# A residual product that reads its projected rows straight from PSUM, in a block of attention and routed experts on one core

## The chip, the cores and the metric

The kernel runs on one core of a Trainium2 chip. The metric is the device time of one launch in microseconds (us), the median of several launches. The engines are named as in the profile: PE (TensorE; PEld is its weight load), DVE (VectorE), ACT (ScalarE), POOL (GpSimd) and SP (SyncE, which here only issues transfers).

## What is computed

Eight sequences of 256 tokens, 256 wide, go through an attention block and a feed-forward block, each between two layer norms and with a residual:

```python
x = x + layernorm(attention(layernorm(x), Wq, Wk, Wv, Wo, b_out))   # 32 heads of 8, 8 key heads, causal, rotary
x = x + layernorm(experts(layernorm(x), ...))                       # top 2 of 8 experts, and 2 shared ones, inner width 640
```

The change lies between the attention's output projection `ctx @ Wo + b_out` and the first residual sum. Because the program centres `Wo` and `b_out` beforehand, the projected rows have mean zero, and the norm needs their mean square alone: `x1 = x + y * (mean(y*y) + eps) ** -0.5`.

## The kernel before

The 2048 tokens are 16 tiles of 128 (index `i`, two for each of 8 sequences). All is in fp32 or in sums of two fp32r or three bf16 parts. Each engine has its own instruction list, and all five lists are written from one list of steps, `plan()`: an engine takes from it the steps that concern it, in that order, and waits on semaphores. So the place of a step in `plan()` sets what it stands behind on every engine that has a part in it. The places come from tables: `FRONT`, `FRONT0`, `FRONT1` for the steps ahead of attention (layer norm, projection, rotary turn, splitting in bf16 parts, transposes by DMA; `FRONT0` is for the first sequence, `FRONT1` for the second), `BACK` for those behind it, `TOPS`, `WHOLE` and `LEAD` for the running start of the maxima, `ORDER` for the order within one of the 64 attention steps. A number in `BACK` is a time in quarters of an attention step. `WARM` gives the number of idle matmuls that PE does behind certain steps of the start.

An attention step `n` is one key head of one sequence with its 4 query heads, 256 by 256 scores. PE makes a first set of scores (`early` and `late`, 7 steps ahead) from which DVE takes the maxima (`tops`, L1078, and `lates`, L1083); POOL turns these into three bf16 parts (`neg`), PE transposes them (`turn`), ACT copies them out and SP writes them beside the queries (`turned`, L1629); then PE makes the scores again with the maxima in them (`pass2`), ACT takes the exponential (`exp`, L930), POOL cuts the causal triangle (L1511), and PE multiplies by the values (`weigh`).

Four steps after a sequence's heads, for each tile `i`, comes what the change touches. PE projects (`b_out`) into a PSUM bank. ACT (`b_taken`) copies the 256 columns to the SBUF tile `YY` and then squares the bank in place with a running sum into `BN`; the bank is free after the squares. POOL (`b_dev`, L1539 and L1541) makes `RS = (sum/256 + eps) ** -0.5`. DVE (`b_add`, L1359) writes `X1 = YY * RS + X1`, and takes the statistics of the second norm (`b_stats2`, L1363, and `b_dev2`, L1366). ACT (`b_norm2`, L948) writes the normalised row to `YY` again, which SP stores for the experts' gather and PE transposes (`b_turn2`) for ACT (`b_high`) and DVE (`b_low`, L1370, tile `XL`).

`banks()` gives out the PSUM banks in the order of `plan()`. During attention the banks 3 to 6 go round as a ring for `early`, `late` (two neighbouring banks), `turn`, `back`, `b_turn`, `b_out`, `b_turn2`, `b_route` and `f_qkv`. PE waits before each until the engine that read the bank last has freed it.

At the start SP issues, from one queue, the transposes by DMA of queries and keys (`q`, L1614, two halves each, and `k`, L1620) and, in the step `k` of the second tile of a sequence, the loads of a later sequence (`XT` L1583, `X` L1579). The first `early` scores need the transposes of tile 0; the first `late` ones need those of tile 0 and of tile 1.

The attention takes the first 250 us of the trace. Behind it PE runs the two shared and the eight routed experts (`up`, `down`), with gathers by POOL's queue.

## Time and profile before

| | us |
|---|---|
| median of 3 launches | 660.78 |
| lowest and highest | 659.98 and 661.0 |
| the profiled launch, as timed | 666.35 |
| its span in the trace | 664.6 |

So 1.75 us of the profiled launch lie around its span, and it was 5.57 us above the median. All positions below are microseconds from the start of the span. Over the span PE was busy for 93%, DVE 80%, ACT 64% and POOL 50%; the mean granted clock of PE was 0.975. A matmul's end is modelled, so PE can show as busy without being at its peak, and an engine's share over the whole span says little here, since attention and experts have different limits: the stretches are to be read one by one. Where a row of the order of time ends in brackets, the engine stood idle before it for so long, and the arrow names what ended it.

### The profile page before, as it was taken

Reading aid. Unit: us, or ns where it says so; the run is one execution under the profiler, and the core shown is the slowest. Engines: PE = TensorE matmul, PEld = TensorE weight load, DVE = VectorE, ACT = ScalarE, POOL = GpSimd, SP = SyncE. Lnnn points to the kernel's source line nnn. Section 1 sums busy time; section 2 is a strip of 40 time slices with the busy share of each in tenths; the row PEclk is TensorE's granted clock in tenths of the full one; section 3 lists DMA queues with packets and bytes.
Section 4 is the critical chain, followed back from the end, with each engine's and each line's share of the span. In section 5 each row is a group of like instructions: output and inputs, shape, how many; then the busy total and the mean of one; then the engine's idle time right before and its main releaser. Section 6 shows DMA issues by size and latency. Waiting matters only on the chain.

```text
span 664.6 us, 14332 instructions
## 1 busy us (share of the span) xinstructions
PE 617.6 (93%) x5400; PEld 514.7 (77%) x5400; DVE 528.7 (80%) x1071; ACT 425.0 (64%) x798; POOL 335.5 (50%) x529
## 2 busy tenths in 40 slices
PE   8778889899989879999979999999999999999995
PEld 6634556566656548888879999999999999888884
DVE  5679999999988734579768888888887888557886
ACT  3436798988988874542256777777876787422222
POOL 3136688787867661100354454545454430078854
PEclk9966899999999999999999999999999999999999
DMA  3973544557450000000375786777776764032311
GB/s 94 158 150 56 99 81 77 120 93 179 100 92 24 13 17 9 17 1 1 126 269 179 242 277 233 242 251 247 240 279 219 265 229 151 25 91 78 97 53 63
DMA packets 79795, 87.08 MB, mean 131 GB/s; under 512 B 54736, under 2 KB 69200, under 8 KB 79728
## 3 DMA queue, kind: packets, MB, share of 16 engines
q0 software_dynamic: 11872, 54.53, 25.0%
q1 hardware_dynamic: 67440, 31.12, 20.8%
q8 instruction: 43, 0.70, 0.4%
q10 hardware_dynamic: 416, 0.52, 0.3%
q14 instruction: 24, 0.20, 0.1%
HBM read 63.87 MB, written 9.31 MB: 110 GB/s over the span
## 4 chain that ended last, share of the span: by engine, by line
PE 66%; DVE 20%; issue 5%; ACT 3%; POOL 3%; another core or an unknown queue 1%; DMA 1%; SPq 0%; POOLq 0%; DVEq 0%; ACTq 0%
PE PS L559 63%; DVE NM L1083 6%; DVE NM L1078 3%; PE PS L768 1%; POOL PF L1511 1%; ACT PF L930 1%; DVE RR L1042 1%; DVE RB L1036 1%; DVE RA L1035 1%; DVE X L1359 1%; PE PS L570 1%; ACT WH L877 1%; DMA WQ<-in_wqkv 1%; DVE RB L1037 1%
## 5 line engine op out<-in xcount | busy, mean ns | idle before, releaser
L1297 DVE TENSOR_TENSOR HF<-SS,PS 128x256 f32<-128x256 f32 (+2 forms) x141 | 68.7, 487 | 72.3 <-PE PS L559 32.6
L1378 DVE TENSOR_TENSOR WL<-RAW,WH 128x768 fp32r<-128x768 f32 x125 | 118.4, 958 | 5.7 <-ACT WH L877 5.2
L976 ACT ACTIVATE SS<-PS 128x256 f32<-128x256 f32 (+2 forms) x141 | 62.0, 439 | 86.7 <-PE PS L559 72.3
L559 PE MATMUL PS<-WH,HH 128*128 128x256 f32 x355 | 103.6, 292 | 3.8 <-DVE HL L1392 2.9
L877 ACT ACTIVATE HH<-HF 128x256 fp32r<-128x256 f32 (+1 forms) x120 | 58.0, 483 | 72.6 <-DVE HF L1297 58.5
L877 ACT ACTIVATE WH<-RAW 128x768 fp32r<-128x768 f32 x125 | 103.4, 841 | 0.0
L1511 POOL TENSOR_SCALAR_AFFINE_SELECT PF<-PF 128x512 f32<-128x512 f32 x128 | 83.9, 679 | 36.5 <-ACT PF L930 36.5
L559 PE MATMUL PS<-WL,HH 128*128 128x256 f32 x355 | 100.3, 283 | 0.0
L559 PE MATMUL PS<-WH,HL 128*128 128x256 f32 x355 | 100.3, 283 | 0.0
L930 ACT ACTIVATE PF<-PS 128x1536 f32<-128x1536 f32 x64 | 92.8, 1450 | 10.8 <-PE PS L559 10.0
L559 PE MATMUL PS<-XGL,WH 128*128 128x256 f32 x320 | 91.0, 284 | 0.0
L559 PE MATMUL PS<-XGH,WH 128*128 128x256 f32 x320 | 90.9, 284 | 0.0
L559 PE MATMUL PS<-XGH,WL 128*128 128x256 f32 x320 | 90.9, 284 | 0.0
L559 PEld LDWEIGHTS PS<-WH,HH 128*128 128x128 f32 x355 | 67.6, 190 | 7.5 <-ACT HH L877 4.1
L1083 DVE TENSOR_REDUCE NM<-PS 128x14 f32<-128x896 f32 x64 | 69.1, 1082 | 4.4 <-PE PS L559 4.0
L559 PEld LDWEIGHTS PS<-WL,HH 128*128 128x128 f32 x355 | 67.5, 190 | 1.9
L559 PEld LDWEIGHTS PS<-WH,HL 128*128 128x128 f32 x355 | 67.7, 191 | 0.0
L1483 POOL DMA_INDIRECT RAW<-in_wa,WIDX x23 | 22.7, 985 | 83.3 <-DVE WL L1378 40.8
L559 PE MATMUL PS<-XH,WH 128*128 128x512 f32 x160 | 64.1, 401 | 0.0
L559 PE MATMUL PS<-XL,WH 128*128 128x512 f32 x160 | 63.3, 396 | 0.0
L559 PE MATMUL PS<-XH,WL 128*128 128x512 f32 x160 | 63.1, 394 | 0.0
L1392 DVE TENSOR_TENSOR HL<-HF,HH 128x256 fp32r<-128x256 f32 (+1 forms) x120 | 62.0, 517 | 0.2 <-ACT HH L877 0.2
(214 smaller groups left out, 1520.2 us busy)
## 6 DMA issues: line engine op xcount, KB each, us to landing
ys<-YO SPq DMA_DIRECT2D x16, 256.0 KB
RAW<-in_wsh SPq DMA_DIRECT2D x4, 768.0 KB, 4.9
XT<-in_xt SPq DMA_DIRECT2D x8, 256.0 KB, 3.4
X<-in_x SPq DMA_DIRECT2D x8, 256.0 KB, 3.3
xn<-YY SPq DMA_DIRECT2D x16, 128.0 KB, 1.7
out<-X SPq DMA_DIRECT2D x15, 128.0 KB
ys<-YO SPq DMA_DIRECT2D x7, 128.0 KB
RAW<-in_wsh SPq DMA_DIRECT2D x2, 384.0 KB, 4.7
```

The source lines that it names most:

```text
L559: return eng.matmul(o, l, r, start=start, stop=stop, skip_group_check=True)
L570: t = eng.transpose(bank(c, 128 * k, 128 * k + 128), src[:, 128 * k:128 * k + 128], idn)
L877: return eng.activation(o, i, ACT.Copy)
L930: eng.activation(PF[:, i % 3, :], PS[:, 0:1536], ACT.Exp, scale=SCALE).then_inc(expd, 1)
L976: eng.activation(ss, both(i, bank(b))[0], ACT.Silu).then_inc(free[b] if dense(i) else silu, 1)
L1078: eng.tensor_reduce(o[:, :, 3:8:2], bank(c, 0, 384).rearrange("p (a v t) -> p a v t", a=2, v=3), AXX, ALU.max, negate=True).then_inc(free[ ...
L1083: eng.tensor_reduce(o[:, :, 9:16], bank(c, 0, 1024).rearrange("p (a v t) -> p a v t", a=2, v=8)[:, :, 0:7, :], AXX, ALU.max, negate=True). ...
L1297: eng.tensor_tensor(hf, ss, both(c, bank(b))[1], ALU.mult).then_inc(free[b], 1)
L1378: eng.tensor_tensor(WL[q % 2][:, c], RAW[raw_of(q)][:, c], WH[q % 2][:, c].bitcast(F32), ALU.subtract).then_inc(w_lo, 1)
L1392: eng.tensor_tensor(HL[:, i % 4, 0:n], HF[:, i % 2, 0:n], HH[:, i % 4, 0:n].bitcast(F32), ALU.subtract).then_inc(h_lo, 1)
L1483: eng.indirect_dma_start(RAW[raw_of(q)][:, 768 * lo:768 * hi], None, (wa, wb, wc)[k], bass.IndirectOffsetOnAxis(ap=WIDX[:, q - 1:q], axis= ...
L1511: eng.affine_select(out=o, in_=o, pattern=[[0, 4], [1, 128]], base=0, channel_multiplier=-1, compare_op=ALU.is_ge, fill=0.0).then_inc(zero ...
```

## The change

ACT's copy of the projected rows goes. Its squares are now written to the upper half of the same bank (columns 256 to 511), so that the lower half keeps the rows; DVE's `b_add` reads them there and frees the bank, which before the squares did. POOL's `b_dev` waits for the squares by their own semaphore. The waits for the room in `YY` go from `b_taken` to `b_norm2`, the step that still writes it. `banks()` keeps a bank out of the ring from `b_out` to `b_add`.

```diff
 elif what == "b_taken":                                    # ACT
     made(e, ("b_out", i))
+    eng.activation(bank(c, 256, 512), bank(c, 0, 256), ACT.Square, accum_out=BN[:, 16 + i, 0:1]).then_inc(b_y, 1)
+elif what == "b_norm2":
+    e.wait_ge(c_nb, i + 1)
     made(e, ("b_turn2", i - 2))
     e.wait_ge(d_xn[i % 2], 16 * (i // 2))
-    copy(YY[:, i % 2, :], bank(c, 0, 256)).then_inc(b_y, 1)
-    eng.activation(bank(c, 0, 256), bank(c, 0, 256), ACT.Square, accum_out=BN[:, 16 + i, 0:1]).then_inc(free[c], 1)
-elif what == "b_norm2":
-    e.wait_ge(c_nb, i + 1)
...
 elif what == "b_add":                                      # DVE
+    c, k = use["b_out", i]
+    made(e, ("b_out", i))
+    e.wait_ge(b_y, i + 1)
     e.wait_ge(b_rs, i + 1)
-    e.wait_ge(b_y, i + 1)
-    eng.scalar_tensor_tensor(out=X1[:, i, :], in0=YY[:, i % 2, :], scalar=RS[:, 16 + i:17 + i], in1=X1[:, i, :],
-                             op0=ALU.mult, op1=ALU.add).then_inc(b_x1, 1)
+    eng.scalar_tensor_tensor(out=X1[:, i, :], in0=bank(c, 0, 256), scalar=RS[:, 16 + i:17 + i], in1=X1[:, i, :],
+                             op0=ALU.mult, op1=ALU.add).then_inc(free[c], 1)
...
 elif what == "b_dev":                                      # POOL
-    read(e, ("b_out", i))
+    e.wait_ge(b_y, i + 1)
...
-LAGS = (9, 10)
+LAGS = (10, 10)
-WARM = {"mean": (9,), "f_qkv": (1, 6, 8, 21), "early": (8, 0, 3, 0, 0, 2, 0), "late": (2,)}
+WARM = {"mean": (14,), "f_qkv": (1, 6, 10, 18), "early": (8, 0, 2, 0, 0, 0, 3), "late": (0,)}
-TOPS = (-8, -7, -7, -5, -5, -2, -1)
+TOPS = (-9, -7, -7, -6, -6, -2, -1)
-ORDER = "a 2 b x d l s1 s0 s2 m0 m1 t w T m2 v W V m3 s3"
+ORDER = "a x 2 b d l s1 s0 m0 s2 t w T m1 v m2 V W s3 m3"
```

The numbers of `FRONT`, `FRONT0`, `FRONT1`, `BACK` and `WHOLE` change too, most of them by one to five. What they move is best seen in the lists of the engines, at the places that the prediction speaks of.

DVE's list in the full middle of attention, once for each tile. `NM` are the maxima (the first of a pair `tops`, the second `lates`), `RA` and `RB` the products of the rotary turn, `XL` the low part of the transposed second norm, `X<-YY,RS,X` the residual product. Before:

```order
L1067 TENSOR_TENSOR KC<-RT,KC 128x8x8
L1078 TENSOR_REDUCE NM<-PS 128x2x3
L1083 TENSOR_REDUCE NM<-PS 128x2x7
L1035 TENSOR_TENSOR RA<-RQ,ROPE 128x320
L1036 TENSOR_TENSOR RB<-RQ,ROPE 128x40x4
L1037 TENSOR_TENSOR RB<-RQ,ROPE 128x40x4
L1334 BN_STATS BN<-X 128x6
L1370 TENSOR_TENSOR XL<-PS,XH 128x2x128
L1337 BN_AGGR MV<-BN 128x2
L1078 TENSOR_REDUCE NM<-PS 128x2x3
L1083 TENSOR_REDUCE NM<-PS 128x2x7
L1359 SCALAR_TENSOR_TENSOR X<-YY,RS,X 128x256
```

The same place after the change:

```order
L1077 TENSOR_TENSOR KC<-RT,KC 128x8x8
L1344 BN_STATS BN<-X 128x6
L1088 TENSOR_REDUCE NM<-PS 128x2x3
L1093 TENSOR_REDUCE NM<-PS 128x2x7
L1347 BN_AGGR MV<-BN 128x2
L1382 TENSOR_TENSOR XL<-PS,XH 128x2x128
L1045 TENSOR_TENSOR RA<-RQ,ROPE 128x320
L1046 TENSOR_TENSOR RB<-RQ,ROPE 128x40x4
L1047 TENSOR_TENSOR RB<-RQ,ROPE 128x40x4
L1371 SCALAR_TENSOR_TENSOR X<-PS,RS,X 128x256
L1088 TENSOR_REDUCE NM<-PS 128x2x3
L1093 TENSOR_REDUCE NM<-PS 128x2x7
```

The low part `XL` and the statistics stand ahead of the rotary products now, and the residual product ahead of the second pair of maxima instead of behind it.

SP's list at the start, from the first transposes on. `XT` and `X` are the loads of the third sequence; `QT` and `KT` are the transposes of tiles 0, 1, 2 in turn. Before:

```order
L1614 DMA_TRANSPOSE QT<-QC 128x16x64 x2
L1620 DMA_TRANSPOSE KT<-KC 128x8x128
L1614 DMA_TRANSPOSE QT<-QC 128x16x64 x2
L1620 DMA_TRANSPOSE KT<-KC 128x8x128
L1583 DMA XT<-in_xt 128x2x256
L1579 DMA X<-in_x 128x2x256
L1614 DMA_TRANSPOSE QT<-QC 128x16x64 x2
L1620 DMA_TRANSPOSE KT<-KC 128x8x128
```

After:

```order
L1626 DMA_TRANSPOSE QT<-QC 128x16x64 x2
L1632 DMA_TRANSPOSE KT<-KC 128x8x128 x2
L1595 DMA XT<-in_xt 128x2x256
L1591 DMA X<-in_x 128x2x256
L1626 DMA_TRANSPOSE QT<-QC 128x16x64 x4
L1632 DMA_TRANSPOSE KT<-KC 128x8x128
```

The two loads and the key transpose of tile 1 stand ahead of the query transpose of tile 1 now; what follows keeps its order.

ACT's list in the middle of attention, at the removed copy. Before:

```order
L930 ACTIVATE PF<-PS 128x1536
L877 ACTIVATE YY<-PS 128x256
L945 ACTIVATE PS,BN<-PS 128x256
L877 ACTIVATE XH<-PS 128x2x128
L877 ACTIVATE NMT<-PS 24x512
L877 ACTIVATE YC<-PS 128x256
L930 ACTIVATE PF<-PS 128x1536
L877 ACTIVATE KC<-KC 128x8x48
```

After:

```order
L941 ACTIVATE PF<-PS 128x1536
L953 ACTIVATE PS,BN<-PS 128x256
L888 ACTIVATE XH<-PS 128x2x128
L888 ACTIVATE NMT<-PS 24x512
L888 ACTIVATE YC<-PS 128x256
L888 ACTIVATE KC<-KC 128x8x48
L941 ACTIVATE PF<-PS 128x1536
```

The copy to `YY` is gone, and the copy `KC` has come ahead of the second exponential.

## Rows read from the trace of the kernel before

**Rows 1.** Stretches: busy us of PE, PEld, DVE, ACT, POOL; PEclk, DMA share, GB/s.

```profile
97.00:123.00 26.00, 23.58 (x314) 15.84 (x318) 25.62 (x55) 22.97 (x43) 21.48 (x44) 1.00 0.53 100
...
276.00:340.00 64.00, 63.31 (x415) 55.23 (x414) 51.25 (x116) 25.00 (x42) 12.79 (x11) 1.00 0.19 61
```

**Rows 2.** DVE lines, 60 to 195 us: ns min/median/max, first and last start.

```profile
L1359 DVE SCALAR_TENSOR_TENSOR X<-YY,RS,X x8: 467/550/765, 95.5 to 184.9; 128x256 f32<-128x256 f32 x8
L1370 DVE TENSOR_TENSOR XL<-PS,XH x8: 400/409/425, 106.1 to 193.9; 128x256 fp32r<-128x256 f32 x8
L1052 DVE TENSOR_TENSOR RT<-RR,QC x10: 407/512/803, 74.2 to 188.2; 128x256 f32<-128x256 f32 x10
```

**Rows 3.** DVE in order of time: start us, duration us, instruction, [idle before].

```profile
132.23 0.52 DVE L1078 TENSOR_REDUCE NM<-PS 128x6 f32<-128x384 f32 x1
132.84 1.09 DVE L1083 TENSOR_REDUCE NM<-PS 128x14 f32<-128x896 f32 x1
133.85 0.48 DVE L1359 SCALAR_TENSOR_TENSOR X<-YY,RS,X 128x256 f32<-128x256 f32 x1
...
144.92 0.52 DVE L1078 TENSOR_REDUCE NM<-PS 128x6 f32<-128x384 f32 x1
...
146.53 0.77 DVE L1359 SCALAR_TENSOR_TENSOR X<-YY,RS,X 128x256 f32<-128x256 f32 x1
```

**Rows 4.** Who waited for whom, 97 to 190 us: sum, times, longest.

```profile
PE PS L559 <- DVE XL L1370: 3.9, 7, 0.6
```

**Rows 5.** POOL in order of time, as rows 3.

```profile
131.75 0.56 POOL L1541 TENSOR_TENSOR RS<-VE,mhalf 128x1 f32<-128x1 f32 x1
...
144.71 0.55 POOL L1541 TENSOR_TENSOR RS<-VE,mhalf 128x1 f32<-128x1 f32 x1
```

**Rows 6.** Groups by line, 97 to 190 us: ScalarE's copy.

```profile
L877 ACT ACTIVATE YY<-PS 128x256 f32<-128x256 f32 x7 | 2.7, 381 | 0.0
```

**Rows 7.** PE in order of time: idle matmuls, centring product, idle ones later.

```profile
1.05 4.21 PE L559 MATMUL PS<-mean 128*128 128x128 f32 x18 [1.05 <-POOL mean L1439]
5.34 2.39 PE L559 MATMUL PS<-WQ,mean 128*128 128x384 f32 x4
...
10.25 0.38 PE L559 MATMUL PS<-mean 128*128 128x128 f32 x2
10.47 1.46 PE L559 MATMUL PS<-WQ,XT 128*128 128x384 f32 x4
```

**Rows 8.** Three stretches, columns as in rows 1.

```profile
0.00:5.00 5.00, 3.95 (x18) 3.92 (x18) 3.05 (x5) 1.49 (x2) 2.28 (x10) 1.00 0.55 160
...
24.00:31.00 7.00, 5.01 (x52) 3.80 (x53) 4.41 (x10) 1.60 (x4) 0.00 (x0) 1.00 0.97 177
76.00:80.00 4.00, 4.00 (x36) 3.18 (x39) 2.63 (x8) 1.36 (x2) 1.47 (x4) 0.66 0.19 32
```

**Rows 9.** SyncE's queue in order of time.

```profile
21.10 3.42 SPq L1614 DMA_TRANSPOSE QT<-QC  x2
24.57 1.96 SPq L1620 DMA_TRANSPOSE KT<-KC  x1
26.57 0.58 SPq L1583 DMA_DIRECT2D XT<-in_xt  x1
...
40.54 1.68 SPq L1629 DMA_DIRECT2D QT<-NMT  x2
```

**Rows 10.** ScalarE waits for the landed query transpose of tile 1.

```profile
27.17 0.84 ACT L877 ACTIVATE QC<-RR 128x768 bf16<-128x768 f32 x1 [2.78 <-DMA QT<-QC]
```

**Rows 11.** PE in order of time: the first late products, then the first pass.

```profile
29.34 0.23 PE L559 MATMUL PS<-CB 64*128 64x128 bf16 x2 [1.63 <-issue]
...
43.97 0.61 PE L559 MATMUL PS<-QT,KT 64*128 64x256 bf16 x2 [1.37 <-DMA QT<-NMT]
```

**Rows 12.** PE in order of time: one tile's projection, twice.

```profile
76.13 2.27 PE L559 MATMUL PS<-WQX,XTX 128*128 128x384 f32 x6
...
126.13 1.30 PE L559 MATMUL PS<-WQX,XTX 128*128 128x384 f32 x6
```

More of the change, by code:

```diff
@@ L49 @@
 NEVER = -1e30
-FRONT = {"f_split": -86, "f_stats": -91, "f_dev": -90, "f_taken": -80, "f_qkv": -77, "f_rope": -75, "f_first": -69,
-         "f_second": -67, "f_third": -61, "q": -59, "k": -56, "k_first": -67, "k_third": -63, "f_fourth": -61,
-         "k_twice": -55}
-FRONT0 = {"f_stats": -105, "f_qkv": -75, "f_dev": -102, "f_taken": -109, "f_rope": -90, "f_third": -76, "f_second":
-          -78, "k_first": -82, "f_first": -82, "q": -72, "k": -69, "k_twice": -72, "k_third": -78, "f_fourth": -74}
-FRONT1 = {"f_dev": -87, "f_stats": -104, "f_rope": -73, "f_first": -73, "f_qkv": -79, "f_taken": -83, "q": -59,
-          "k_first": -72, "f_second": -69, "k": -55, "f_third": -62, "k_third": -67, "f_fourth": -58, "k_twice": -52}
-BACK = {"b_turned": 47, "b_turn": 45, "b_add": 56, "b_out": 53, "b_stats2": 59, "b_norm2": 66, "b_dev": 53, "b_dev2":
-        60, "b_turn2": 70, "b_route": 75, "b_taken": 53, "b_low": 70, "b_high": 68, "b_kept": 75}
-TOPS = (-8, -7, -7, -5, -5, -2, -1)
-WHOLE = (-7, -7, -6, -4, -3, -2, -1)
-ORDER = "a 2 b x d l s1 s0 s2 m0 m1 t w T m2 v W V m3 s3"
+FRONT = {"f_split": -87, "f_stats": -93, "f_dev": -91, "f_second": -65, "f_qkv": -77, "f_taken": -78, "f_rope": -74,
+         "f_first": -69, "f_third": -61, "q": -59, "k": -56, "k_third": -63, "k_twice": -57, "k_first": -67,
+         "f_fourth": -61}
+FRONT0 = {"f_stats": -112, "f_qkv": -73, "f_dev": -102, "f_taken": -114, "f_rope": -89, "f_third": -78, "k_first":
+          -83, "f_second": -80, "q": -70, "f_first": -83, "k": -69, "k_twice": -71, "k_third": -79, "f_fourth": -77}
+FRONT1 = {"f_dev": -81, "f_stats": -103, "f_first": -74, "f_rope": -80, "f_qkv": -82, "f_taken": -82, "q": -55,
+          "k_first": -78, "f_second": -70, "k": -54, "k_third": -70, "f_third": -61, "k_twice": -57, "f_fourth": -62}
+BACK = {"b_turned": 47, "b_turn": 44, "b_add": 55, "b_out": 53, "b_stats2": 58, "b_dev": 53, "b_norm2": 67, "b_dev2":
+        60, "b_route": 75, "b_turn2": 68, "b_taken": 53, "b_low": 68, "b_kept": 72, "b_high": 70}
+TOPS = (-9, -7, -7, -6, -6, -2, -1)
+WHOLE = (-7, -7, -5, -4, -4, -2, -1)
+ORDER = "a x 2 b d l s1 s0 m0 s2 t w T m1 v m2 V W s3 m3"
 PICKS = ((0, 14), (14, 2))
@@ L263, in banks @@
 def banks(stages):
+    held = {"b_add": "b_out"}
     use, after, lates, pair, count, ring, crossed = {}, {}, {}, {}, [0] * 8, [3, 4, 5, 6], 0
+    allowed, kept = (3, 4, 5, 6), []
     for s in stages:
         if s[0] == "ring":
-            ring = list(s[1])
+            allowed = s[1]
+            ring = [b for b in allowed if b not in kept]
         elif s[0] in ("mean", "f_qkv", "early", "late", "turn", "back", "b_turn", "b_out", "b_turn2", "b_route"):
@@ L285, in banks @@
                 after[s] = wide
+                if s[0] in held.values():
+                    ring.remove(b)
+                    kept.append(b)
+        elif s[0] in held:
+            b = use[held[s[0]], s[1]][0]
+            kept.remove(b)
+            if b in allowed:
+                ring.append(b)
         elif s[0] == "up" and not DENSE <= s[1] < LAST:
@@ L477, in build @@
         wq_h, wq_l, xt_h, xt_l = (sem(n) for n in ("wq_h", "wq_l", "xt_h", "xt_l"))
-        b_y, b_ve, b_rs, b_x1 = (sem(n) for n in ("b_y", "b_ve", "b_rs", "b_x1"))
+        b_y, b_ve, b_rs = (sem(n) for n in ("b_y", "b_ve", "b_rs"))
         c_st, c_mv, c_ve, c_rs, c_x2, c_xh, c_nb = (sem(n) for n in ("c_st", "c_mv", "c_ve", "c_rs", "c_x2", "c_xh", "c_nb"))
@@ L1356, in _ @@
                 elif what == "b_add":
+                    c, k = use["b_out", i]
+                    made(e, ("b_out", i))
+                    e.wait_ge(b_y, i + 1)
                     e.wait_ge(b_rs, i + 1)
-                    e.wait_ge(b_y, i + 1)
-                    eng.scalar_tensor_tensor(out=X1[:, i, :], in0=YY[:, i % 2, :], scalar=RS[:, 16 + i:17 + i], in1=X1[:, i, :],
-                                             op0=ALU.mult, op1=ALU.add).then_inc(b_x1, 1)
+                    eng.scalar_tensor_tensor(out=X1[:, i, :], in0=bank(c, 0, 256), scalar=RS[:, 16 + i:17 + i], in1=X1[:, i, :],
+                                             op0=ALU.mult, op1=ALU.add).then_inc(free[c], 1)
                 elif what == "b_stats2":
-                    e.wait_ge(b_x1, i + 1)
+                    read(e, ("b_out", i))
                     eng.bn_stats(BN[:, 32 + i, :], X1[:, i, :]).then_inc(c_st, 1)
```

## The prediction

> **What bounds the kernel now.** First the stretches: in the middle of attention DVE is busy for 25.62 of 26.00 us, while PE, ACT and POOL all have room [rows 1]. So there, from about 50 to 190 us, the time is DVE's list, plus any hole in it. From 276 us on PE is busy for 63.31 of 64 us [rows 1], and nothing that the change touches is late. Between these, from 190 to 250 us, the chain of waits goes round PE, ACT's exponential and POOL's causal cut. Ahead of 50 us the chain goes over the first transposes by DMA, and every later step hangs on these. Three terms follow: the saving in DVE's list, what takes its place there, and the start.
>
> **ACT's copy goes.** It took 381 ns a tile [rows 6], 16 x 0.381 = 6.1 us in all. In the middle ACT is busy for 22.97 of 26.00 us [rows 1], so DVE's list hides it: 0. In the stretch from 190 to 250 us some five of the copies lie, 5 x 0.38 = 1.9 us at the most, but behind most of them ACT waits for PE or POOL; I take 0, and keep -1.9 as the lower end.
>
> **DVE reads PSUM.** The product took 467 ns at best, 765 at worst, median 550 [rows 2]; in two tiles that follow each other it took 0.48 and 0.77 [rows 3]. Instructions with both inputs in SBUF spread like that (407 to 803 ns for RT), one with an input in PSUM does not (400 to 425 ns, XL), with POOL as busy beside both [rows 2]. No row has this instruction with an input in PSUM. XL and RT have the same best time, so PSUM adds nothing, and I take 0.47: a saving of (0.48 + 0.77) / 2 - 0.47 = 0.155 a tile. Eight tiles lie where DVE is the bound: -1.2. The bounds are 0 and 8 x (0.77 - 0.40) = -3.0.
>
> The Trainium skill, "SBUF — State Buffer", section "Who interferes with whom", has the reason for the spread: a VectorE instruction with two SBUF inputs and a GpSimd instruction that reads SBUF lock each other out. By that rule, the trace agrees (803 against 425 ns). Against the change speaks "VectorE: DVE Perf Modes" of the Trainium skill, section "The TRN2 errata": a VectorE instruction has a fixed 120 cycles from PSUM against 58 from SBUF, an estimate of 65 ns more. By it the saving would be 8 x 0.09 = 0.7 us; the 400 against 407 ns of the trace do not show it, and I go by them.
>
> **XL goes ahead of the rotary products.** In the middle PE waited seven times for XL, up to 0.6 us [rows 4], since the bank is wanted for the next late product. DVE pays a part: the second maxima start 0.61 us after the first (132.23 to 132.84), which take 0.52, and elsewhere an instruction starts 0.08 before the one ahead of it ends (133.85 against 132.84 + 1.09) [rows 3]. So 0.61 - 0.44 = 0.17 us are a hole. XL now runs some 1.7 us earlier, and the hole goes: 7 x 0.17 = -1.2; bounds 0 and -1.2.
>
> **The residual product goes ahead of the pair of maxima.** That puts a wait for POOL's RS in DVE's list, with both maxima queued behind it, and behind those PE's banks. RS was ready at 131.75 + 0.56 = 132.31 and at 144.71 + 0.55 = 145.26 [rows 5]; the place that the product now has came at 132.23 and 144.92 [rows 3]. So the hole is 0.08 and 0.34, mean 0.21, x 8 = +1.7 if all else stays. POOL gains a little: DVE's product no longer shuts it out, and the rotary products come later beside its causal cut. I take 0.16 x 8 = +1.3; bounds 0 and 8 x 0.5 = +4.0. Holding the bank until b_add costs nothing that I see: its next user is a later step's `back`, behind the place where DVE has passed the product.
>
> Middle of attention: -1.2 - 1.2 + 1.3 = -1.1, with bounds of some -4 and +2.
>
> **The start: five more idle matmuls.** Nine of them (18 passes) ran from 1.05 to 5.26 us, and the centring product began at 5.34 when the weights were there [rows 7]. So nothing hides five more. A pass took 4.21 / 18 = 0.23 us there, and 0.11 later (two in the 0.22 us from 10.25 to the next product at 10.47); the stretch from 0 to 5 is marked with a full granted clock all the same [rows 7, 8], so the speed is to be read from durations. The product too ran slowly, 2.39 us for four where four of that shape took 1.46 at 10.47 [rows 7]. Ten more passes cost 2.3 us at 0.23 and 1.1 at 0.11; the product behind them wins back up to 0.9 when it falls in the fast part. I take +1.0; bounds +0.3 and +2.3.
>
> **The start: two loads ahead of the query transpose of tile 1.** Before, that transpose was issued from 21.10 to 24.52 and had landed at 27.17, 2.65 later [rows 9, 10]; the key transpose was issued until 26.53 [rows 9], and with its landing PE began the late products at 29.34 after 1.63 us of idle [rows 11]. Now the order is key, loads, query. The queue's sum up to the last of the two grows by the two issues, 0.58 + 0.5, so they are complete 1.1 us later. That is the least: the DMA engines were busy for 0.97 of that stretch at 177 GB/s [rows 8], where 512 KB are 2.9 us. I take +1.1, as the issue and not the transfer set the pace of the queue; upper end +2.9. DVE wins back about 0.5 behind it, as the statistics and a key product no longer stand between the late maxima and the third query. The next thing is SP's write of the maxima at 40.54 [rows 9], on which the first pass waited until 43.97 [rows 11]; it moves with DVE's list: +1.1 - 0.5 = +0.6. Taken together the start costs 1.0 + 0.6 = +1.6, bounds +0.3 and +4.5. The other counts in `WARM` move by three or fewer, in idle time.
>
> **Sum.** -1.1 + 1.6 = +0.5, tail 0. The profiled launch, 666.35 with a span of 664.6, becomes 666.85 and 665.1. The median lies 5.57 below the profiled launch; scaled, 660.78 becomes 661.3. I put it at 661.2.
>
> **Rivals.** *The gain stays.* POOL's power comes just in time (the 0.08 of one tile in two, not the 0.34), and the wait at the start is less: the weights land later than in the profiled launch, so that the idle matmuls are hidden. For it: RS needs only 0.1 to 0.3 us; and DVE's other instructions with two SBUF inputs, up to 803 ns, may fall better beside POOL. Against: the idle matmuls filled the wait for the weights to 0.08 us. -1.2 - 1.2 + 0.3 + 0.3 = -1.8, with the tail's copies -2.3: 658.5.
>
> *Slower: the loads before the query transpose.* If the transfer and not the issue sets the pace, tile 1 is complete 2.9 and not 1.1 us later: +2.4 behind DVE's part, +1.0 for the idle matmuls, -1.1 in the middle: +2.3, 663.1. It decides from 2 us of added delay at the first late product. For it speaks the share of 0.97 [rows 8]; against it that the loads are plain copies of large rows, and that the transposes were issued one behind the other at their own pace.
>
> *The clock.* PE granted 0.66 between 76 and 80 us, where one tile's projection took 2.27 us against 1.30 at a clock of 1.00 [rows 8, 12], and DVE stood idle behind it. The low clock, 1.2 of 2.4 GHz, came after PE had waited for DVE and DMA. A shift of the start can put one projection more or fewer under it: about 1 us either way, 660.2 or 662.2.
>
> *The change does nothing but the start.* The holes in DVE's list change places and the middle gives 0: +1.6, 662.4; I count it with the slower case.
>
> **Chances.** The forecast, start and middle cancelling to within 1.3 us: 0.36 (0.03 of it faster, 0.29 the same, 0.04 slower). The gain stays: 0.30, faster. Slower by the start: 0.24. The clock: 0.10 (0.02, 0.05, 0.03). A measurement tells about 0.2%, 1.3 us, from no change. Faster 0.35, same 0.34, slower 0.31. The range takes in both rivals' times but not their far ends: 658.3 to 663.5.
>
> **What would show it.** The product at about 0.47 us in every tile, without the 0.77; no wait of PE for XL in the middle; DVE waiting for RS in front of the product, 0.1 to 0.3 us for most tiles; the first late product later than 29.34 by 2, the first pass later than 43.97 by 1.6; the centring product later than 5.34. Wrong would be: a product above 0.53 us (PSUM costs); the first pass at 44 or earlier (the start is free); waits for RS above 0.4 us or PE waiting for the bank of the product; a stretch from 190 to 250 us that is shorter by more than 1 us.

## The result: slower by 0.65% on one chip, by 0.15% on another

| | us |
|---|---|
| kernel after, median of 5 launches | 663.75 (663.01 to 667.31) |
| kernel before, median of 5 on the same chip | 659.98 (659.01 to 661.0) |
| ratio | 1.0065, interval 1.0034 to 1.0095 |
| the profiled launch of after; its span | 664.62; 662.9 |

The time lay 0.25 us above the upper end of the range, and the kernel was slower where the forecast was no change. The profiled launch of before (666.35 us) had been an unusually long one. So I took three more traces of before and three of after, and all distances below are means of four traces of each.

The sum is read best from one instruction that both kernels have 64 times, ACT's exponential of an attention step. These are its 1st, 14th, 44th and 64th start, start and duration (ACT in order of time, columns as [rows 3]). In before:

```profile
45.10 1.45 ACT L930 ACTIVATE PF<-PS 128x1536 f32<-128x1536 f32 x1 [1.70 <-PE PS L559]
...
90.66 1.45 ACT L930 ACTIVATE PF<-PS 128x1536 f32<-128x1536 f32 x1
...
185.99 1.45 ACT L930 ACTIVATE PF<-PS 128x1536 f32<-128x1536 f32 x1 [0.42 <-PE PS L559]
...
242.80 1.45 ACT L930 ACTIVATE PF<-PS 128x1536 f32<-128x1536 f32 x1 [0.37 <-PE PS L559]
```

In after:

```profile
46.07 1.45 ACT L941 ACTIVATE PF<-PS 128x1536 f32<-128x1536 f32 x1 [1.23 <-PE PS L570]
...
87.18 1.45 ACT L941 ACTIVATE PF<-PS 128x1536 f32<-128x1536 f32 x1
...
185.39 1.45 ACT L941 ACTIVATE PF<-PS 128x1536 f32<-128x1536 f32 x1 [0.77 <-PE PS L570]
...
242.85 1.45 ACT L941 ACTIVATE PF<-PS 128x1536 f32<-128x1536 f32 x1 [0.37 <-PE PS L570]
```

| stretch, mean of 4 traces | before | after | difference |
|---|---|---|---|
| start to 1st exponential | 44.8 | 46.0 | +1.15 |
| 1st to 14th | 44.9 | 41.3 | -3.6 |
| 14th to 44th | 95.4 | 98.1 | +2.65 |
| 44th to 64th | 56.8 | 57.4 | +0.63 |
| to the 64th, sum | 241.9 | 242.75 | +0.85 |

The 14th to 44th exponential, seven and a half tiles, is the stretch to trust: over four traces it ran from 95.24 to 95.70 us before and from 97.96 to 98.21 after. The granted clock was 1.00 there in all eight traces.

The 1st to 14th (43.6 to 45.7 us before, 41.0 to 41.6 after) is mixed with the granted clock, which differs between the two kernels. In the first trace of before, then of after (columns as [rows 1], granted clock third from the end):

```profile
45.10:90.66 45.56, 38.13 (x436) 22.61 (x431) 41.89 (x86) 33.16 (x49) 29.75 (x54) 0.82 0.44 85
```

```profile
46.07:87.18 41.11, 32.85 (x436) 20.38 (x436) 39.59 (x91) 32.75 (x48) 29.38 (x54) 0.95 0.49 95
```

Over four traces it was 0.82 to 0.88 before and 0.91 to 0.99 after.

So attention ends less than 1 us later, and yet the medians are 3.8 us apart. The rest lies in the experts, in instructions that the change did not touch; that comes last below.

**The middle of attention after the change.** The stretch of after that answers to the first of [rows 1]:

```profile
97.00:123.00 26.00, 24.46 (x318) 15.94 (x322) 23.95 (x57) 22.95 (x42) 20.80 (x43) 1.00 0.51 96
```

The line of the product in after, 60 to 195 us, that answers to [rows 2]:

```profile
L1371 DVE SCALAR_TENSOR_TENSOR X<-PS,RS,X x9: 484/484/484, 91.4 to 194.8; 128x256 f32<-128x256 f32 x9
```

The product takes 0.484 us in every tile, and the 0.77 is gone, as forecast. But DVE, which was busy for 25.62 of 26 us, is busy for 23.95, and the time from one tile to the next is longer all the same. It stands still for something now. Who waited for whom in after, 97 to 190 us, DVE's part (us in all, times, longest):

```profile
DVE X L1371 <- POOL RS L1553: 3.8, 7, 0.6
DVE XL L1382 <- ACT XH L888: 2.3, 6, 0.5
```

PE's part, to be held against [rows 4]:

```profile
PE PS L825 <- DVE NM L1093: 3.0, 7, 0.6
PE PS L570 <- DVE X L1371: 2.4, 2, 1.3
```

In before DVE had one wait of 0.2 us in all there. DVE in order of time in one tile of after, against [rows 3]:

```profile
128.13 0.43 DVE L1382 TENSOR_TENSOR XL<-PS,XH 128x256 fp32r<-128x256 f32 x1 [0.34 <-ACT XH L888]
...
129.00 0.31 DVE L1046 TENSOR_TENSOR RB<-RQ,ROPE 128x160 f32<-128x160 f32 x1
129.24 0.31 DVE L1047 TENSOR_TENSOR RB<-RQ,ROPE 128x160 f32<-128x160 f32 x1
130.10 0.48 DVE L1371 SCALAR_TENSOR_TENSOR X<-PS,RS,X 128x256 f32<-128x256 f32 x1 [0.55 <-POOL RS L1553]
130.50 0.55 DVE L1088 TENSOR_REDUCE NM<-PS 128x6 f32<-128x384 f32 x1
```

What POOL did there:

```profile
127.51 1.23 POOL L1523 TENSOR_SCALAR_AFFINE_SELECT PF<-PF 128x512 f32<-128x512 f32 x2 [0.39 <-ACT PF L941]
...
129.22 0.75 POOL L1553 TENSOR_TENSOR RS<-VE,mhalf 128x1 f32<-128x1 f32 x1
```

And PE:

```profile
130.73 0.23 PE L570 MATMUL PS<-CB 64*128 64x128 bf16 x2 [1.13 <-DVE X L1371]
```

The chain in this tile reads: the causal cut ends at 128.74, POOL makes RS from 129.22 to 129.97, DVE stands idle for 0.55 us and starts the product at 130.10, the maxima come behind it, and PE, whose next late product wants the pair of banks with the projected rows in it, has been idle for 1.13 us by 130.73. PE waits for the product in every third tile (two waits between 97 and 190 us); in the others it waits for the maxima. The two `RB` take 0.31 us each, where they took 0.76 and 0.75 in the kernel before. That was not in my sum.

**The start.** PE in after, the rows that answer to [rows 7]:

```profile
1.04 5.65 PE L570 MATMUL PS<-mean 128*128 128x128 f32 x28 [1.04 <-POOL mean L1451]
6.53 1.46 PE L570 MATMUL PS<-WQ,mean 128*128 128x384 f32 x4
9.15 1.53 PE L570 MATMUL PS<-WQ,XT 128*128 128x384 f32 x4 [1.16 <-DVE WQ L1341]
```

SyncE's queue in after, against [rows 9]:

```profile
19.28 3.13 SPq L1632 DMA_TRANSPOSE KT<-KC  x2
22.46 0.58 SPq L1595 DMA_DIRECT2D XT<-in_xt  x1
...
23.61 7.65 SPq L1626 DMA_TRANSPOSE QT<-QC  x4
```

PE in after at the first late product and the first pass, against [rows 11]:

```profile
30.39 0.29 PE L570 MATMUL PS<-CB 64*128 64x128 bf16 x2 [2.94 <-DMA QT<-QC]
...
44.94 0.61 PE L570 MATMUL PS<-QT,KT 64*128 64x256 bf16 x2
```

The trace of before that I had read was untypical here: its centring product took 2.39 us, in the three others 1.56, 1.56 and 2.12. Means of four traces, before and after: first projection at 8.41 and 8.96, so the stretch with the idle matmuls grew by 0.55 us; first late product 20.29 and 21.25 us behind it, so the stretch with the two loads ahead of the query transpose grew by 0.96; first pass at 43.79 and 44.85, +1.06. No run moved the idle matmuls or the loads alone, so that these two moves are the cause is read from the order of the rows.

### The profile page after: what moved, and what is told of

Read it like the earlier page. It is cut to its first block, busy times and chain, and to the rows that moved or that the text cites. A ratio compares the mean times of both kernels' runs of the same rounds, so it can differ in the third digit from the quotient of the medians.

```text
span 662.9 us, 14328 instructions
## 1 busy us (share of the span) xinstructions
PE 615.5 (93%) x5404; PEld 513.9 (78%) x5404; DVE 519.7 (78%) x1071; ACT 421.3 (64%) x782; POOL 333.2 (50%) x529
## 4 chain that ended last, share of the span: by engine, by line
PE 69%; DVE 11%; POOL 7%; ACT 6%; issue 3%; SPq 2%; DMA 1%; another core or an unknown queue 1%; POOLq 0%; DVEq 0%; ACTq 0%
PE PS L570 66%; DVE NM L1093 4%; POOL PF L1523 4%; ACT PF L941 3%; DVE NM L1088 2%; PE PS L779 1%; PE PS L581 1%; POOL RS L1553 1%; SPq L1632 1%; DMA QT<-QC 1%; SPq L1626 1%; ACT WH L888 1%; DVE X L1371 1%; ACT YY L958 1%
## 5 line engine op out<-in xcount | busy, mean ns | idle before, releaser
L1523 POOL TENSOR_SCALAR_AFFINE_SELECT PF<-PF 128x512 f32<-128x512 f32 x128 | 79.9, 648 | 45.0 <-ACT PF L941 44.5
L1495 POOL DMA_INDIRECT RAW<-in_wa,WIDX x23 | 24.0, 1044 | 85.4 <-DVE WL L1390 43.2
```

The costliest lines, as they stand in the source:

```text
L1495: eng.indirect_dma_start(RAW[raw_of(q)][:, 768 * lo:768 * hi], None, (wa, wb, wc)[k], bass.IndirectOffsetOnAxis(ap=WIDX[:, q - 1:q], axis= ...
L1523: eng.affine_select(out=o, in_=o, pattern=[[0, 4], [1, 128]], base=0, channel_multiplier=-1, compare_op=ALU.is_ge, fill=0.0).then_inc(zero ...
```

## The experiments

What they were to tell apart: (1) the held bank costs, since PE's late product waits for it; (2 and A) the product's wait for RS ahead of the maxima costs; (B) the new place of XL costs; (3) the start costs. Later came (C), the places of XL and of the product act together, and (R), the rest of the difference is chance or the chip. The runs lie on five chips, A to E; ratios are to the kernel before on the same chip; the distance is from the 14th to the 44th exponential, where before has 95.4 and after 98.1.

### The kernel before again

> The kernel before, once more, for a second trace beside the one with a launch of 666.35 us. If that trace was long by the granted clock alone (0.67 from 50 to 64 us, while the kernel after had 0.88 there), this one has its 14th exponential about 3 us earlier than 90.66 us, and the same distance of 95.3 us from the 14th to the 44th exponential. If the middle itself varies from launch to launch, that distance is another one. Time: 660 us, ratio 1.000.

Chip A, ratio 1.0002 (0.9984 to 1.0020), distance 95.5, 14th exponential at 89.73. So the middle repeats to 0.2 us, and the 14th exponential came 0.9 us earlier, not the 3 us expected. Of the 5.2 us between the two traces 2.65 lay in the experts' hole (below) and 1.8 behind it, not in the clock of attention, as I had supposed.

### The order without the code

All code as before, all nine tables of numbers as after; of these:

```diff
-LAGS = (9, 10)
+LAGS = (10, 10)
...
-ORDER = "a 2 b x d l s1 s0 s2 m0 m1 t w T m2 v W V m3 s3"
+ORDER = "a x 2 b d l s1 s0 m0 s2 t w T m1 v m2 V W s3 m3"
```

> The new tables of order with the old code: ACT copies the rows to SBUF and frees the bank with its squares, DVE multiplies from SBUF. Theory 1, the held bank: in the kernel after PE's late product waits 1.1 to 1.3 us for the residual product, because its bank pair holds the projected rows, and this costs 0.38 us a tile from 88 to 186 us. Then this kernel has no such wait, the middle period falls from 13.1 to 12.8 us a tile, and it is some 3 us faster than the kernel after: 660 to 661.5 us, ratio 1.000 to 1.002. Theory 2, the wait of DVE for RS in front of the maxima: it is here too, so 663 to 664 us, ratio 1.005 to 1.006. Theory 3, the start: it is here too, also 663 to 664 us, but the distance from the 14th to the 44th exponential is 95.3 us and not 98.2 us.

Chip A, ratio 1.0065 (1.0046 to 1.0084), distance 98.1. The held bank is not the cause: here ACT frees it with its squares, and the middle is as long as with the new code. The product, from SBUF, takes 484 ns here too. With this order the code is worth nothing, either way.

### The code without the order

All code as after, all nine tables as before; against the kernel after:

```diff
-LAGS = (10, 10)
+LAGS = (9, 10)
...
-ORDER = "a x 2 b d l s1 s0 m0 s2 t w T m1 v m2 V W s3 m3"
+ORDER = "a 2 b x d l s1 s0 s2 m0 m1 t w T m2 v W V m3 s3"
```

> The new code (product from PSUM, bank held until it, no copy) with all tables of order as before. The product stands behind the maxima of the step, and the late product of that step takes the pair of banks that the second transposed scores and the early product of the same step had last, so PE waits there for the first maxima of that step and not for the residual product. Theory 1, the held bank: the ring of four is a ring of three for longer, about 4 us a tile, and this kernel is the slowest, 664 to 667 us, ratio 1.006 to 1.010; the gain of 0.155 us a tile in DVE's product shows but is not seen in the time. Theory 2 (the cost is DVE's wait for RS ahead of the maxima): the product waits for nothing here, so 659 to 660.5 us, ratio 0.998 to 1.000.

Chip A, ratio 1.0118 (1.0095 to 1.0141), distance 100.9, a little more than theory 1 said. So the code costs 5.5 us in the middle where the product stands behind the maxima. The product itself took 473 to 475 ns in all eight tiles.

### The old start under the new middle

The kernel after with `WARM`, `LAGS`, `FRONT0` and `FRONT1` of before:

```diff
-LAGS = (10, 10)
+LAGS = (9, 10)
-WARM = {"mean": (14,), "f_qkv": (1, 6, 10, 18), "early": (8, 0, 2, 0, 0, 0, 3), "late": (0,)}
+WARM = {"mean": (9,), "f_qkv": (1, 6, 8, 21), "early": (8, 0, 3, 0, 0, 2, 0), "late": (2,)}
...
```

> The kernel after with the tables of the first two sequences and the idle matmuls as before (WARM, FRONT0, FRONT1, LAGS). Theories 1 and 2, the loss lies in the middle: 662.5 to 664 us, ratio 1.004 to 1.006, distance from the 14th to the 44th exponential 98.2 us. Theory 3, the start: 659 to 660.5 us, ratio 0.998 to 1.001.

Chip A, ratio 1.0071 (1.0056 to 1.0086), 664.85 us against 662.5 to 664 expected, distance 98.9. Putting the start back gains nothing. Its first exponential came at 48.85, later than in either kernel, I suppose because `TOPS` and `WHOLE` no longer fit the tables of the start, and its granted clock was below 1.00 in the middle (0.98); so this run says that the start is not the cause, not what it costs.

### The new start over the old middle

The kernel before with the same four tables of after:

```diff
-LAGS = (9, 10)
+LAGS = (10, 10)
-WARM = {"mean": (9,), "f_qkv": (1, 6, 8, 21), "early": (8, 0, 3, 0, 0, 2, 0), "late": (2,)}
+WARM = {"mean": (14,), "f_qkv": (1, 6, 10, 18), "early": (8, 0, 2, 0, 0, 0, 3), "late": (0,)}
...
```

> The kernel before with the tables of the first two sequences and the idle matmuls of the kernel after (WARM, FRONT0, FRONT1, LAGS); code and middle as before. If the new start is worth what the traces show from the first to the 14th exponential (41.1 and 41.5 us in two kernels with the new tables, 44.6 and 45.6 before) less the first exponential coming 1.0 us later, and the middle keeps its 95.4 us, this kernel has its 44th exponential at 182.5 to 184 us and takes 657.5 to 659 us, ratio 0.996 to 0.998: it beats both. If that gain came from the granted clock of two lucky launches or from the new middle tables, it takes 660.5 to 662 us, ratio 1.001 to 1.002.

Chip B, ratio 1.0032 (1.0012 to 1.0053), distance 95.3, first exponential at 47.86. A miss: a gain was expected, and the new start is none by itself.

### The product ahead of the maxima, alone

```diff
-BACK = {... "b_add": 56, ...}
+BACK = {... "b_add": 55, ...}
```

> The kernel before with one number changed: b_add at 55 in place of 56, so that DVE's residual product (from SBUF, as before) stands ahead of a pair of maxima and waits for RS there. Theory A, the product's wait for RS is what lengthens the middle: the distance from the 14th to the 44th exponential grows from 95.4 us by 1.5 to 2.6 us, to 97 to 98 us, with a wait of DVE for RS in each tile; time 662 to 663 us, ratio 1.003 to 1.004. Theory B, the earlier place of XL is: the distance stays at 95.4 us and the time at 660 us.

Chip B, ratio 1.0027 (1.0010 to 1.0044), distance 96.3, and 1.9 us more from the 44th to the 64th. DVE's wait in this kernel, 92 to 184 us:

```profile
DVE X L1359 <- POOL RS L1541: 1.9, 5, 0.6
```

1.9 us in 5 of 7 tiles, 0.27 a tile: the wait is there, near the size that the prediction read from [rows 3] and [rows 5]. It costs, less than the 1.5 to 2.6 us of theory A, and alone it does not make the loss of the kernel after.

### XL ahead of the rotary products, alone

```diff
-FRONT = {... "f_rope": -75, ...}
+FRONT = {... "f_rope": -74, ...}
```

> The kernel before with one number changed: f_rope at -74 in place of -75, so that XL stands ahead of the three rotary products in DVE's list, as in the kernel after, while the residual product stays behind the maxima. Theory A: PE's wait for XL (3.9 us in 7 times) goes, the distance from the 14th to the 44th exponential is 95.4 us or up to 1.3 us less. Theory B: DVE waits for ACT's XH in front of XL, 0.3 to 1.0 us a tile, and the distance grows to 97 to 98 us, ratio 1.003 to 1.004.

Chip B, ratio 0.9932 (0.9906 to 0.9957), distance 93.2: one number, 4.5 us faster. Again, on chip E:

> The kernel before with f_rope at -74 once more. The attention part ended 3.8 us earlier in its trace (64th exponential at 238.3 against 242.0 us). If that is all, the ratio is 0.993 to 0.995 whatever the chip; if part of the 4.5 us measured first came from the hole in the experts, it lies between 0.995 and 0.998 on another chip.

Ratio 0.9929 (0.9913 to 0.9945), 655.14 against 659.62 us, distance 92.9. The gain is real, and almost four times what I had forecast for this move; neither theory had it. Where it lies, by line of DVE from 97 to 190 us (busy us, mean ns | idle before). In the kernel before:

```profile
L1036 DVE TENSOR_TENSOR RB<-RQ,ROPE 128x160 f32<-128x160 f32 x7 | 5.3, 755 | 0.0
L1035 DVE TENSOR_TENSOR RA<-RQ,ROPE 128x320 f32<-128x320 f32 x7 | 4.4, 633 | 0.0
...
L1037 DVE TENSOR_TENSOR RB<-RQ,ROPE 128x160 f32<-128x160 f32 x7 | 3.9, 561 | 0.0
```

With f_rope at -74:

```profile
L1035 DVE TENSOR_TENSOR RA<-RQ,ROPE 128x320 f32<-128x320 f32 x7 | 3.3, 471 | 0.0
...
L1037 DVE TENSOR_TENSOR RB<-RQ,ROPE 128x160 f32<-128x160 f32 x7 | 2.3, 323 | 0.0
L1036 DVE TENSOR_TENSOR RB<-RQ,ROPE 128x160 f32<-128x160 f32 x7 | 2.2, 318 | 0.0
```

The same three instructions take 1.11 us a tile and not 1.95. In order of time, this kernel's DVE:

```profile
126.63 0.42 DVE L1370 TENSOR_TENSOR XL<-PS,XH 128x256 fp32r<-128x256 f32 x1 [0.69 <-ACT XH L877]
126.97 0.48 DVE L1035 TENSOR_TENSOR RA<-RQ,ROPE 128x320 f32<-128x320 f32 x1
...
127.60 0.32 DVE L1037 TENSOR_TENSOR RB<-RQ,ROPE 128x160 f32<-128x160 f32 x1
```

And its POOL:

```profile
125.74 1.23 POOL L1511 TENSOR_SCALAR_AFFINE_SELECT PF<-PF 128x512 f32<-128x512 f32 x2 [0.40 <-ACT PF L930]
...
127.58 0.75 POOL L1541 TENSOR_TENSOR RS<-VE,mhalf 128x1 f32<-128x1 f32 x1
```

DVE waits 0.69 us for XH in front of XL, so the rotary products begin when POOL's causal cut is over, and lie beside two instructions on one column. In the kernel before they lay beside the cut: `RB` from 130.13 to 131.56, the cut from 129.95 to 131.39. The cut itself took 1.44 us there and takes 1.23 here. The other side shows at RS: 0.75 us beside the rotary products, 0.56 [rows 5] beside XL. So theory B had the wait right (0.7 us a tile) and the sign wrong: from the 14th to the 44th exponential DVE was idle for 6.9 us against 1.8 in the second trace of before, and busy for 86.3 against 93.7. The wait is repaid by more than itself.

### Both moves

```diff
-FRONT = {... "f_rope": -75, ...}
+FRONT = {... "f_rope": -74, ...}
-BACK = {... "b_add": 56, ...}
+BACK = {... "b_add": 55, ...}
```

> The kernel before (product from SBUF) with two numbers changed: f_rope at -74 (XL ahead of the rotary products; alone it gave 93.2 us from the 14th to the 44th exponential and 655.6 us) and b_add at 55 (the product ahead of the maxima; alone 96.3 us and 661.6 us). Theory C, the two meet: with the rotary products short, DVE reaches the product's place some 0.5 us before RS is there, so the wait is now in every tile and eats the whole gain: 97 to 98 us, 663 us, ratio 1.004 to 1.006, as the kernel with all new tables (98.1). Theory D, the two add up: 93.2 + 0.8 = 94 us, 657.5 us, ratio 0.996; then something else in the new tables costs the other 4 us.

Chip C, ratio 1.0005 (0.9992 to 1.0018), distance 97.7: theory C in the middle, though not in the time (659.0 us, and 663 expected; the 1st to 14th exponential kept the gain of the f_rope move, 41.8 us). On top of the f_rope move, b_add costs 4.7 us in the middle, alone 0.8. DVE's waits in this kernel, 92 to 184 us:

```profile
DVE XL L1370 <- ACT XH L877: 4.8, 7, 1.0
DVE X L1359 <- POOL RS L1541: 2.8, 7, 0.4
```

And one of PE's:

```profile
PE PS L559 <- DVE NM L1078: 3.4, 8, 0.6
```

The product waits in all seven tiles, 2.8 us in all, and the wait passes on: PE's products wait for the first maxima (`L1078`), 3.4 us. In the kernel with f_rope alone that wait is not there.

The wait for RS is not the whole of the 4.7 us: it comes to some 3.0 over seven and a half tiles. The rest is in part the price of another place beside POOL. The sum `RR`, behind the product in DVE's list and with both inputs in SBUF, lies longer beside POOL's product `XTX` now. From 92 to 184 us, with f_rope alone:

```profile
L1042 DVE TENSOR_TENSOR RR<-RA,RB 128x320 f32<-128x320 f32 x8 | 5.4, 672 | 0.0
```

And with both moves:

```profile
L1042 DVE TENSOR_TENSOR RR<-RA,RB 128x320 f32<-128x320 f32 x7 | 6.0, 863 | 0.0
```

With all new tables it is 570 ns with the product at its old place, in the next section, and 946 with it at the new one.

### The new order with the product at its old place

Code as before, all tables as after but one number:

```diff
-BACK = {... "b_add": 55, ...}
+BACK = {... "b_add": 56, ...}
```

> Old code with all new tables, but b_add at 56 as before. Theory C, b_add's place is what turns the gain of the new tables into a loss: the distance from the 14th to the 44th exponential falls from 98.1 to 93 to 94 us and the time to 655.5 to 658 us, ratio 0.993 to 0.997. Theory D, other moves of the new tables cost it: 97 us or more, 662 to 663 us.

Chip C, ratio 0.9969 (0.9949 to 0.9988), distance 93.7: theory C again. One number turns the loss of 98.1 into a gain. Again, on chip E beside f_rope alone:

> Old code, all new tables, b_add at 56, once more, beside the kernel with f_rope alone. The 64th exponential stood at 239.1 us against 238.3 us there, and the hole at 43.7 against 45.5 us: the two within 0.2% of each other, 0.993 to 0.997.

Ratio 0.9981 (0.9959 to 1.0003), distance 94.3: a miss. It is slower than f_rope alone there by 2.8 us, and no gain clear of noise; the other new numbers together cost rather than add.

### The new code with XL early

Code as after, all tables as before but one number:

```diff
-FRONT = {... "f_rope": -75, ...}
+FRONT = {... "f_rope": -74, ...}
```

> The new code (product from PSUM, bank held, no copy) with the old tables and f_rope at -74. Theory 1, holding the bank costs 5.4 us from the 14th to the 44th exponential wherever the product stands behind the maxima (100.9 against 95.5 with all old tables): 98 to 99.5 us here, 662 to 664 us, ratio 1.003 to 1.006. If the loss of the held bank was hidden behind DVE's list and shows only in that one order: 93 to 94 us and 655 to 657 us.

Chip C, ratio 1.0026 (1.0011 to 1.0041), distance 99.1, where the old code had 93.2. The middle is as theory 1 said (98 to 99.5). The time, 660.3 us, is lower than its 662: in the trace the 1st to 14th exponential took 40.5 us, and the experts' hole (below) had its shortest form.

### Holding the bank, alone

The new code with the old tables, the copy put back and the product reading it; of the new code changed:

```diff
 elif what == "b_taken":
+    copy(YY[:, i % 2, :], bank(c, 0, 256)).then_inc(b_cp, 1)
     eng.activation(bank(c, 256, 512), bank(c, 0, 256), ACT.Square, ...)
 elif what == "b_add":
-    eng.scalar_tensor_tensor(..., in0=bank(c, 0, 256), ...).then_inc(free[c], 1)
+    eng.scalar_tensor_tensor(..., in0=YY[:, i % 2, :], ...).then_inc(free[c], 1)
```

> The new code with the old tables, but with the copy to SBUF back on ACT and the product reading it, while the bank is still held until the product. What differs from the kernel before is the held bank (and the squares in its upper half); what differs from the new code with old tables is the copy and the product's source. Theory 1, the held bank costs and not the reading of PSUM: 101 to 102.5 us from the 14th to the 44th exponential, as with the new code and old tables (100.9), PE waiting for the first maxima 1 us a tile, 667 to 670 us. Rival, PSUM or the missing copy is what moved it: 95 to 96 us, 660 us.

Chip C, two launches, ratio 1.0100 (1.0065 to 1.0134), distance 101.0 against 100.9 with the new code and old tables. The middle is as theory 1 said, the time, 665.0 us, 2 us below its 667. So neither the source of the product nor the missing copy moves the middle; the held bank does (the squares in the upper half are common to both kernels too, and PE's wait speaks for the bank). The source does move the product: from SBUF it took 530 to 806 ns at this place, median 604, and from PSUM, in the new code with old tables, 473 to 475. PE's longest sum of waits in this kernel, 92 to 184 us:

```profile
PE PS L570 <- DVE NM L1091: 7.5, 7, 1.2
```

With a bank out of the ring, the late product gets the bank that the early product of the same step had just filled, and waits for the maxima from it (L1091, the first maxima), 1.1 us a tile.

### More traces of both kernels

> The kernel after once more, for a second trace. The distance from the 14th to the 44th exponential is 98.2 us again, the 64th at 243 us. The two traces of the kernel before differ by 2.65 us in one hole, where PE waits for the first gathered weights at 340 to 347 us and then runs at half the clock; the trace of the kernel after had the long form. If the long form is chance, this one has the short form about every second time, and launches lie at 660 and 663 us; if the kernel after always has the long form, its launches lie at 663 to 664 us throughout. Ratio 1.0065 again.

Chip B: ratio 1.0073 (1.0046 to 1.0100), distance 98.0, long hole (48.6 us).

> The kernel after, third trace. Theory H, it meets the long form of the hole for a reason: the stretch from the 12th to the 23rd product HF is 48 to 49 us again, launches 662.5 us or more, ratio 1.0065. Theory R, chance or the chip: the stretch has any length from 43.7 to 48.6 us, some launches lie near 659.5 to 660.5 us, and the ratio comes nearer to the 1.001 that the 64th exponential alone would give.

> The kernel before, third trace. Theory H: the stretch is 43.7 to 46 us. Theory R: any length from 43.7 to 48.6 us. The 14th to the 44th exponential 95.4 us in both.

> The kernel after, fourth trace, for the same question: 48 to 49 us by theory H, any length by theory R.

> The kernel before, fourth trace, for the same question: 43.7 to 46 us by theory H, any length by theory R.

Chip D: after 660.07, before 659.03, ratio 1.0015 (1.0003 to 1.0027); before against itself 1.0005. The hole was 43.7 us in both traces of after and 45.0 and 44.8 in those of before: theory R.

**The hole in the experts.** The stretch from the 12th to the 23rd product `HF` (DVE, L1297 of before, 304 to 352 us) is 43.7 us long at best. Elsewhere behind the 64th exponential the traces of the two kernels agree to 0.6 us (the first profiled launch of before lost 1.8 us more there). In it ACT and PE wait for a transfer; the only ones under way are POOL's gathers (976 of the 977 packets from 330 to 352 us in after). ACT's row at the longer wait, in after on chip B:

```profile
344.78 0.38 ACT L986 ACTIVATE SS<-PS 128x256 f32<-128x256 f32 x1 [5.32 <-remote]
```

In after on chip D:

```profile
341.57 0.39 ACT L986 ACTIVATE SS<-PS 128x256 f32<-128x256 f32 x1 [0.96 <-PE PS L570]
```

In the first ACT stands idle for 5.32 us for something that the profile doesn't name, in the second for 0.96 us for PE alone. The chain of waits (start, us, what) in the first trace of after, with the 24 products behind that wait:

```profile
340.06 5.30 another core or an unknown queue
...
346.98 4.61 PE PS L570 x24
```

The same products in the second trace of before:

```profile
340.41 0.87 another core or an unknown queue
...
344.73 3.10 PE PS L559 x24
```

After the longer wait PE runs the 24 products in 4.61 us for 3.10, at the lower clock. The stretches from 345 to 350 us (columns as [rows 1], granted clock third from the end), in after:

```profile
345.00:350.00 5.00, 3.02 (x15) 3.05 (x16) 2.80 (x6) 2.84 (x6) 0.00 (x0) 0.72 0.48 177
```

And in the second trace of before, at the full 2.4 GHz:

```profile
345.00:350.00 5.00, 5.00 (x44) 5.00 (x43) 4.69 (x11) 3.10 (x7) 0.94 (x1) 1.00 0.46 173
```

So a late landing costs twice, by the wait and by the clock, up to 4.9 us here. A shorter wait comes a little earlier: in all four traces of before PE stands still for 0.7 to 1.1 us ahead of the transpose of gathered tokens, in none of after. In the third trace of before:

```profile
333.52 0.66 PE L768 MATMUL PS<-CF,XG 128*128 128x128 f32 x4 [1.11 <-DMA XG<-xn,XIDX]
```

In the two traces of before on chip D, where it is the only such wait, the stretch is 1.1 and 1.3 us longer than the 43.7 of after. Put together: in the first trace of after and on chip B after had 48.5 and 48.6 us in the stretch, before 48.6 in its first trace and 46.0 on chip A; on chip D after had 43.7 twice, before 45.0 and 44.8. If before stands mostly at 46.0 on such chips as A and B (one trace on A says so, and none of before was taken on B), that is +2.6 against -1.2 on D, and this swing of 3.8 us is about the swing of the ratio, from 1.0065 and 1.0073 to 1.0015. With the +0.85 of attention the first comes to +3.45, measured +3.8 to +4.5; chip D, where attention was 1.6 apart, to +0.4, measured +1.0. So traces and launches agree to about a microsecond, and no closer. Over all kernels the stretch was 45.4 to 48.6 us on A and B, 43.7 to 45.0 on C and D, 45.5 and 46.0 on E.

## Why the prediction was wrong, step by step

**The forecast was 661.2, and no change; measured 663.75.** The attention part came near its sum (+0.5 forecast, +0.85 measured at the 64th exponential), but that is luck: two terms, the place of XL and the place of the product, were both far too small and of opposite sign. The step "tail 0" failed.

- *Tail 0.* This is the step that put the time outside the range. Attention explains 0.85 of the 3.8 us between the medians; the rest, some 3 us, lies behind it, in instructions that are the same in both. In the traces the hole was 2.6 us longer in after on B than in before on A, and 1.2 us shorter on chip D; in the first pair of traces it was equally long (48.5 and 48.6), so the place is worked out from the others and not shown launch by launch. I had read only one trace, and one row of busy time (63.31 of 64 us, [rows 1]) which ends before the hole. I had seen that the profiled launch was 5.6 us above the median, and scaled by it instead of asking where it lay: in this hole, behind it, and in the low clock of the start.
- *ACT's copy.* Right: worth nothing. The copy put back with the bank held moved the middle by 0.1 us; in the new order the old code, with the copy, has 98.1 as the new code has.
- *DVE reads PSUM, 0.47 us, saving 0.155 a tile.* The duration was right: 0.484 in every tile. But there are two ways to end the 0.77, and the forecast had only one. At the old place it is the source, as I had said: 473 to 475 ns from PSUM, 530 to 806 from SBUF (the two kernels with the bank held). At the new place the source no longer matters: from SBUF the product takes 483 to 487 ns too. And the saving did not show in the time: the middle took 100.9 us with the product from PSUM and 101.0 from SBUF in the old order, 98.1 from either in the new one. The Trainium skill's "VectorE: DVE Perf Modes", section "The TRN2 errata", by which I had estimated 65 ns more from PSUM, is not borne out here: undisturbed products took 473 to 475 ns from PSUM (new code, old tables) and 467 at best from SBUF, and 484 from either at the new place.
- *XL ahead of the rotary products, -1.2 (bounds 0 and -1.2).* With the next one the largest mis-sized term. Measured alone: -2.4 us from the 14th to the 44th exponential, some -3.3 before, +1.2 behind, together 4.5 us of the launch. Part of the -3.3 goes with the granted clock; at an equal one (0.87, the first trace with f_rope at -74 and the third of before) it is -1.6. I priced the hole of 0.17 us which the move closes and not the three instructions that it moves out from beside the causal cut, although I had named the spread (407 to 803 ns) and its reason two paragraphs earlier. And I did not see that XL would wait for XH.
- *The residual product ahead of the maxima, +1.3 (bounds 0 and +4.0).* Right in kind: DVE waits for RS. Alone it had about the size forecast (+0.8 in the middle, 0.27% or 1.8 us of the launch). But I added it to the term before as if they were independent. With the rotary products 0.84 us shorter, DVE reaches the product early, and RS takes 0.75 instead of 0.56 beside them: the wait is 0.40 us a tile with both moves and 0.54 in the kernel after, above the 0.4 that I had named as a sign of being wrong, and the term is +4.7 in the middle with `RR`. The sum of the bounds was wrong as well: by its own terms the middle could reach +4.0, not +2.
- *Holding the bank costs nothing.* Right for the order as changed (98.1 with and without), wrong as said in general: PE did wait for the product (2.4 us in two waits, 1.3 the longest), and in the old order the held bank costs 5.5 us. I had said that the bank's next user is a later `back`. By `banks()` that holds for most tiles of the kernel after, but in every third one (tiles 0, 3 and 6) it is a late product, and there PE waits.
- *The start, +1.6.* +1.15 measured. The stretch with the idle matmuls grew by 0.55 and not 1.0, since the centring product behind them then runs at full speed in every trace (1.46 us); the stretch with the two loads by 0.96, forecast 1.1, at the pace of the queue's issues. The rival "loads before the query transpose" (2.9 us) did not come.
- *The clock.* The first 14 steps vary by 2.1 us between four launches of the kernel before, and the mean granted clock there was 0.82, 0.88, 0.87 and 0.82, against 0.95, 0.99, 0.92 and 0.91 after. So the clock is a difference between the two, in favour of after, and goes with the -3.6 us of this stretch. How much of that it makes, and how much the shorter waits do, no run tells: the start's new tables alone had 0.92 and 43.2 us.

None of the rivals was the one that came. "The gain stays" is what the order gives once b_add is put back: 656.1 us on chip C, and 657.9 on E, where before has 659.6.

## What to carry to other kernels

Moving VectorE's SBUF products out from beside GpSimd's long instructions was worth more than the hole in the list that I had counted, even at the price of a new wait; but a step that gains time ahead of a wait hands it to the wait, so moves in one list don't add up. A buffer that is freed later also changes who gets the others of its ring, and the cost stands where one of them then meets a late reader: print the users again after every move. Before pricing 0.2%, take several traces of the kernel before on more than one chip, since unchanged code differed by up to 4.9 us here.
